# Relational layer: first half multiplied by quarters, turns one place later, ScalarE normalising a half later

## The reference

```python
B, N, D_IN, D_OUT, R = (8, 1024, 128, 128, 4)
rel_ids = jnp.arange(1, weight.shape[0] + 1, dtype=relation.dtype)
masks = (relation[None] == rel_ids[:, None, None, None]).astype(x.dtype)
h = jnp.einsum('rbnm,bmd->rbnd', masks, x)
y = jnp.einsum('rbnd,rdo->bno', h, weight)
y = y + bias
...
x = _layernorm(x + y, axis=-1)     # (x - mean) / sqrt(var + 1e-5)
```

## Time and profile before

| | |
|---|---|
| median of 3 runs | 127.29 us |
| the profiled execution, whole | 128.38 us |
| its span, first to last instruction | 126.6 us |
| PE busy | 104.6 us (83%) |
| DVE busy | 96.2 us (76%) |
| ACT busy | 83.4 us (66%) |
| POOL busy | 79.8 us (63%) |
| moved by DMA | 42.15 MB, 333 GB/s over the span |

### The profile page before, as it was taken

The page is one execution under the profiler, slowest core; times in us unless marked ns, Lnnn a source line. Parts: engine busy times, 40 slices in busy tenths (PEclk is TensorE's granted clock), DMA queues, the critical chain, the costliest instruction groups (busy, mean ns, idle before and its releaser), DMA issues.

```text
span 126.6 us, 1876 instructions
## 1 busy us (share of the span) xinstructions
PE 104.6 (83%) x551; PEld 85.0 (67%) x559; DVE 96.2 (76%) x243; ACT 83.4 (66%) x114; POOL 79.8 (63%) x76
## 2 busy tenths in 40 slices
PE   5933399989999789899999999999999999997100
PEld 2312288687878567678887887788879886896000
DVE  0249925277949999999999999999999997639820
ACT  4056780766649178699589939994999499951400
POOL 6008000067253989899989989999999899043510
PEclk9996557999999999999999999999999999999855
DMA  4999999999999999999999999999999700400620
GB/s 116 409 422 430 425 422 432 422 430 405 434 419 419 427 417 425 410 436 417 422 365 409 425 422 359 421 427 427 388 281 418 311 18 0 166 0 0 250 87 8
DMA packets 7362, 42.15 MB, mean 333 GB/s; under 512 B 819, under 2 KB 1206, under 8 KB 3254
## 3 DMA queue, kind: packets, MB, share of 16 engines
q1 hardware_dynamic: 7350, 42.01, 81.7%
HBM read 37.82 MB, written 4.19 MB: 332 GB/s over the span
## 4 chain that ended last, share of the span: by engine, by line
DMA 25%; DVE 22%; PE 18%; ACT 11%; POOL 11%; issue 6%; SPq 2%; DVEq 0%; POOLq 0%; ACTq 0%
DMA adj_sb<-in_adj_dram 25%; PE h_ps L187 13%; POOL scale L217 10%; ACT maskT L355 9%; DVE mask L426 6%; DVE stats L205 4%; DVE var_eps L214 4%; DVE total L440 3%; PE tp_ps L178 2%; PE y_ps L199 2%; DVE mean_var L210 2%; DVE out_sb L221 2%; ACT out_sb L374 1%; ACT h_sb L362 1%; SPq L244 1%
## 5 line engine op out<-in xcount | busy, mean ns | idle before, releaser
L355 ACT ACTIVATE maskT<-tp_ps 128x2048 fp32r<-128x2048 fp8e5 x32 | 59.7, 1873 | 8.1 <-PE tp_ps L178 8.1
L426 DVE TENSOR_SCALAR mask<-adj_sb 128x2048 uint8<-128x2048 uint32 x32 | 39.7, 1266 | 16.2 <-DMA adj_sb<-in_adj_dram 16.1
L217 POOL TENSOR_TENSOR scale<-var_eps,power 128x4 f32<-128x4 f32 (+1 forms) x17 | 44.3, 2608 | 0.6 <-DVE var_eps L214 0.6
L187 PE MATMUL h_ps<-maskT,x_hi 128*128 128x512 f32 (+1 forms) x136 | 35.7, 406 | 1.1 <-ACT maskT L355 0.9
L187 PE MATMUL h_ps<-maskT,x_lo 128*128 128x512 f32 (+1 forms) x136 | 33.8, 391 | 0.0
L178 PEld LDWEIGHTS tp_ps<-identity,mask 128*128 128x128 f32 x128 | 20.3, 204 | 13.8 <-DVE mask L426 10.2
L187 PEld LDWEIGHTS h_ps<-maskT,x_hi 128*128 128x128 f32 x136 | 24.7, 197 | 6.6 <-ACT maskT L355 2.3
L178 PE MATMUL tp_ps<-identity,mask 128*128 128x128 f32 x128 | 22.3, 300 | 7.9 <-DVE mask L426 7.8
L374 ACT ACTIVATE out_sb<-total,shift,scale 128x128 f32<-128x128 f32 x31 | 13.7, 488 | 19.8 <-POOL shift L319 19.8
L187 PEld LDWEIGHTS h_ps<-maskT,x_lo 128*128 128x128 f32 x136 | 23.5, 189 | 3.9
L199 PE MATMUL y_ps<-w_sb,h_sb 128*128 128x128 f32 x128 | 17.3, 277 | 1.6 <-ACT h_sb L362 1.3
(11 more groups left out here) (32 smaller groups left out, 33.3 us busy)
## 6 DMA issues: line engine op xcount, KB each, us to landing
adj_sb<-in_adj_dram SPq DMA_DIRECT2D x32, 1024.0 KB, 12.2
x_sb<-in_x_dram SPq DMA_DIRECT2D x8, 512.0 KB, 5.9
out_dram<-out_sb SPq DMA_DIRECT2D x7, 512.0 KB, 16.5
out_dram<-out_sb SPq DMA_DIRECT2D x1, 256.0 KB, 2.4
out_dram<-out_sb SPq DMA_DIRECT2D x2, 128.0 KB, 1.9
w_sb<-in_L_gnn_weight_dram SPq DMA_DIRECT2D x1, 64.0 KB, 6.5
bias_rows<-in_L_gnn_bias_dram SPq DMA_DIRECT2D x3, 0.5 KB
```

Of the source, the lines that this page charges most:

```text
L187: last = nc.tensor.matmul(h_ps[:, bank, 0:n], (x_hi, x_lo)[part][:, slot, t, :], maskT[:, places, t // WORD, t % WORD, :], start=(first an ...
L217: nc.gpsimd.tensor_tensor(scale[:, slot, tiles], var_eps[:, slot, tiles], power[:, tiles], ALU.pow).then_inc(done, by)
L355: nc.scalar.activation(maskT[:, u % NMT], turned_codes(u % NTP), ACT.Copy, accum_out=counts[:, u:u + 1]).then_inc(expanded, 1)
L426: nc.vector.tensor_scalar(mask[:, u % NMASK], adj_sb[:, u % NADJ].bitcast(u32), CAP, SET, ALU.min, ALU.mult).then_inc(masked, 1)
```

## The change

Several things move, and no arithmetic on the data is added or taken away.

- PE in the loop: a turn now stands behind the products that it stood ahead of. The order is hi_products(hf), turn(2hf+3), project_half(hf-1), lo_products(hf), turn(2hf+4).
- ACT: finish_half is that of half hf-3 instead of hf-2, and at the end the finishes stand between the copies.
- DVE: each pair of converts is one unit earlier in number (2hf+4 and 2hf+5), so that add and measure of a half stand ahead of one more convert. `find_others` stands ahead of the last whole add, and the flag is written ahead of the two last adds. `place_bias` stands ahead of convert(1).
- Half 0 goes by quarters: each quarter is multiplied behind its own turn, copied and projected before half 1 starts. Two stretches of idle matmuls (8 and 4) on a zero tile are added.
- `x_hi` and `x_lo` of batch 0 are made by POOL.
- The bias and the weight are loaded from ACT's queue, not SP's; x of the next batch is loaded one unit later.
- At the end PE's order is: first part of quarter 0, projection of half 14, second part of quarter 0, first part of quarter 1, the sum of counts, projection of quarter 0, second part of quarter 1, projection of quarter 1.

```diff
-            load_unit(1)
-            sp.wait_ge(bias_cleared, 1)
-            for q in PARTS:
-                sp.dma_start(bias_rows[q:q + 1, :], bias.unsqueeze(0)).then_inc(bias_loaded, 16)
-            sp.dma_start(w_sb[:, 0, :], weight[0]).then_inc(weights_loaded, 16)
-            for u in range(2, UNITS):
+            for u in range(1, UNITS):
                 load_unit(u)
-                if u % CH == 1 and u // CH + 1 < B:
+                if u % CH == (2 if u >= CH else 3) and u // CH + 1 < B:
                     load_batch(u // CH + 1)
-                if u == 3:
-                    load_batch(1)
...
             split_bias()
+            hi(0)
+            lo(0)
...
+            act.wait_ge(bias_cleared, 1)
+            for q in PARTS:
+                act.dma_start(bias_rows[q:q + 1, :], bias.unsqueeze(0)).then_inc(bias_loaded, 16)
+            act.dma_start(w_sb[:, 0, :], weight[0]).then_inc(weights_loaded, 16)
             expand(0)
-            act.wait_ge(topped, 1)
-            nc.scalar.activation(flat(x_hi[:, 0]), flat(x_top[:, :]).bitcast(fp32), ACT.Copy).then_inc(hi_made, 1)
             expand(1)
-            for hf in range(HALVES - 1):
-                if hf >= 1:
+            copy_quarter(0, 0)
+            expand(2)
+            copy_quarter(0, 1)
+            expand(3)
+            for hf in range(1, HALVES - 1):
+                if hf >= 2:
                     copy_half(hf - 1)
                 expand(2 * hf + 2)
                 expand(2 * hf + 3)
-                if hf >= 2:
-                    finish_half(hf - 2)
+                if hf >= 3:
+                    finish_half(hf - 3)
             copy_half(HALVES - 2)
+            finish_half(HALVES - 4)
+            copy_quarter(HALVES - 1, 0)
             finish_half(HALVES - 3)
-            copy_quarter(HALVES - 1, 0)
             copy_quarter(HALVES - 1, 1)
...
             convert(0)
             top(0)
-            convert(1)
-            dve.wait_ge(topped, 1)
-            take_lo(nc.vector, 0, 0, lo_made)
-            convert(2)
             place_bias()
-            convert(3)
+            for u in (1, 2, 3):
+                convert(u)
+            top(1)
             convert(4)
-            for hf in range(HALVES - 1):
-                for u in (2 * hf + 5, 2 * hf + 6):
+            convert(5)
+            for hf in range(1, HALVES - 1):
+                for u in (2 * hf + 4, 2 * hf + 5):
...
+            find_others()
             add_half(HALVES - 2)
             measure_half(HALVES - 2)
             finish_half(HALVES - 3)
-            find_others()
+            dve.wait_ge(flag_counted, 1)
+            nc.vector.tensor_copy(flag[:, :], tp_ps[0:1, 0, 0:1]).then_inc(flag_ready, 1)
...
             turn(0)
+            keep_warm(8)
+            hi_quarter(0, 0)
             turn(1)
+            lo_quarter(0, 0)
             turn(2)
-            for hf in range(HALVES - 1):
+            hi_quarter(0, 1)
+            lo_quarter(0, 1)
+            turn(3)
+            pe.wait_ge(weights_loaded, 16)
+            pe.wait_ge(bias_split, 4)
+            project_half(0)
+            keep_warm(4)
+            hi_products(1)
+            turn(4)
+            lo_products(1)
+            turn(5)
+            turn(6)
+            for hf in range(2, HALVES - 1):
+                hi_products(hf)
                 if 2 * hf + 3 < UNITS:
                     turn(2 * hf + 3)
-                hi_products(hf)
+                project_half(hf - 1)
+                lo_products(hf)
                 if 2 * hf + 4 < UNITS:
                     turn(2 * hf + 4)
-                if hf == 1:
-                    pe.wait_ge(weights_loaded, 16)
-                    pe.wait_ge(bias_split, 4)
-                if hf >= 1:
-                    project_half(hf - 1)
-                lo_products(hf)
-            products_quarter(HALVES - 1, 0)
+            hi_quarter(HALVES - 1, 0)
             project_half(HALVES - 2)
-            products_quarter(HALVES - 1, 1)
-            project_quarter(HALVES - 1, 0)
+            lo_quarter(HALVES - 1, 0)
+            hi_quarter(HALVES - 1, 1)
             pe.wait_ge(flag_step, 2)
             nc.tensor.matmul(tp_ps[0:1, 0, 0:1], above[:, 1:2], ones[:, 0:1], start=True, stop=True).then_inc(flag_counted, 1)
+            project_quarter(HALVES - 1, 0)
+            lo_quarter(HALVES - 1, 1)
             project_quarter(HALVES - 1, 1)
```

21 lines of the change are left out of this document (11 added, 10 removed).

## The result

The changed kernel takes 120.25 us, median of four executions (118.53 to 121.04), beside 127.31 us (126.42 to 127.34, four executions) for the kernel before on the same chip. The ratio is 0.9365, with a 95% interval of 0.927 to 0.946.

A forecast was written before the change was run, and what follows sets the result against it. Bound by data up to 37 us, by full DVE to 101.5, then DVE waits for PE. Start 1.8, loop nothing, end the rest: 5.0 summed, 4.9 taken, so 127.29 - 4.9 = 122.4 us, range 120.8 to 125.5.

The forecast's parts named there:

- The start: Data-bound stage: DVE work moves ahead of convert(10), convert(11) starts at 39.4 instead of 41.4; 1.8 us gained.
- The bias rival: Start, DVE: place_bias waits for a late bias ahead of 31 converts; 129 us, chance 0.05 including other slower causes.
- order of issue: Start, DMA: if loads land as issued, bias at about 15.5 and convert(1) at 19.4; the sum stays the same.
- The start has enough slack for the rest: Start: POOL's batch 0 work, half 0 by quarters, 12 idle matmuls and two PE waits cost nothing.
- The loop: From 37 to 101.5 us: DVE stays full at 12.0 us per batch, so nothing is gained.
- this sign (a period below 11.8): Loop, DVE: a batch period below 11.8 us would mean x_lo has slid off var_eps.
- The end: From add 12: PE in time, DVE's 1.73 us wait before add 13 goes, 0.35 of 2.01 stays before add 14.
- the walk: Timing of DVE and PE through the end, instruction by instruction: last finish at 116.3 instead of 121.22, 4.9 us.
- What follows the last finish: After DVE's last finish: the store, its landing and the end were claimed to stay, so no gain.
- ACT's finish is only the loudest wait: Loop: ACT's 19.8 us wait for POOL's shift stands beside a full DVE and does not set the stage's length.
- More than counted: unit 11 early: Start and end: unit 11 is there by 37.5 and PE keeps up; 120.5 to 121 us, chance 0.07.

The follow-up runs named there:

- the long execution: Second profiled execution of the changed kernel, nothing further edited: 120.83 us, span 119.1, DVE batches of 11.97 us.
- the short one: First profiled execution of the changed kernel, nothing further edited: 118.53 us, span 116.7, two DVE batches of 11.15 us.

## Why the prediction was off

**The start** held. convert(11) was at 39.3 and 39.5 for 39.4; x_lo met it in the long execution as written (until 40.9 was forecast, until 41.02 it was), and in the short one came behind it, at 41.03, and met var_eps instead (0.70). The bias rival did not come: place_bias began at 8.0 in the short execution and ended at 12.2, and a beginning at 20.0 was still in time by the prediction, as the timeline of all engines shows:

```profile
6.79 0.40 POOL L287 TENSOR_TENSOR bias_rest<-bias_rows 128x128 f32<-128x128 f32 x1 [4.15 <-DMA bias_rows<-in_L_gnn_bias_dram]
...
8.03 1.22 DVE L491 COPY bias_parts<-bias_rows 1x512 bf16<-1x512 bf16 x1 [0.29 <-POOL bias_fine L290]
9.27 2.49 DVE L491 COPY bias_parts<-bias_rest 1x512 bf16<-1x512 bf16 x1
...
12.22 2.36 DVE L429 TENSOR_SCALAR mask<-adj_sb 128x2048 uint8<-128x2048 uint32 x2
```

The bias landed at 6.8 on ACT's queue; it was 9.5 behind unit 1 before. The 15.5 that the prediction gave for order of issue had a wrong premise: ACT issued the bias from 1.50 to 2.6, when SP was at units 1 (1.72) and 2 (2.19), not behind unit 3. Its last piece was still issued behind unit 1 and landed 2.6 us ahead of where unit 1 landed before (9.4). By the Trainium skill, "DMA: Bandwidth & Descriptors", "Queues, rings and completion order", the engines take turns between queues: the trace agrees, 6.8.

"The start has enough slack for the rest ... I cost them at nothing" holds only where DVE sets the loop, as in the long execution. Where PE sets it, its start comes through to add 14 one to one, and in the chains of those traces PE's start goes back to convert(1) and the bias copies ahead of it. By the place of place_bias alone the median moves by 1.7 to 2.7 us, in part by more short executions.

**The loop** was costed at nothing, by two steps. "Turns one place later are needed by converts that are one unit lower in number, so that this cancels" hid that the turns' place is what keeps the converts' lead: the converts alone are worth nothing, with the turns 4 us. Whoever had taken the converts' move as the gain would have been wrong by all of it. "The 1.3 us per batch that x_lo costs through var_eps stays" is the first step that failed. The order on POOL does stay, but the amount doesn't: it is 1.28 us (1.45 - 0.17) in the long execution and 0.48 in the short one's first batches, since the pow ahead of x_lo gets through sooner or later between two converts. The prediction named this sign (a period below 11.8) and gave it no chance. With where x_lo falls at convert(11) it makes the 2.44 us between the two executions. It explains little of the median's miss if the six of ten executions at 120.6 to 121.0 are long ones, of which one was profiled. What decides whether an execution is long or short is not settled.

**The end** held: no wait ahead of add 13, 0.76 ahead of add 14 for the 0.35 written, the last finish 0.26 us ahead of its time in the long execution. 5.18 us came up to there, for the 4.9 of the walk.

**What follows the last finish** is the step that put the forecast out of its range. "What follows the last finish (the store, its landing, the end) stays" was taken as 5.4 us; it was 3.06. The flag's move was priced as the 0.1 to 0.2 us of its instruction on DVE, and not by what waits for the flag: five engines that read it and branch. On the long execution the two add up to what was measured, as they must, being read from it: 128.38 - 5.18 - 2.3 = 120.9, for 120.83. Without this term it would have been 123.2, beside the 123.5 forecast. From the median the forecast's own 4.9 and this term give 127.3 - 4.9 - 2.3 = 120.1, for 120.25; that it comes so close is partly luck, since the median lies between the two kinds of execution.

**The rivals.** That ACT's finish is only the loudest wait was held and shown. "More than counted: unit 11 early" gave 120.5 to 121, close to the right time for a wrong reason: unit 11 came at 39.3, not 37.5.

## What to carry to other kernels

Price an instruction that is moved by who waits for its result, the end of the program included: here 0.14 us on DVE stood for 2 us of five engines' endings. Two moves that form one ring through PE and DVE have to be judged together: the converts alone showed nothing, and with the turns 4 us. Where two engines are both nearly full, write down both paces (here 11.5 us per batch for PE, 11.15 or 11.97 for DVE), since removing one wait only brings up the other. And where two engines hold each other up at the scale of a tenth of a microsecond, give the period a range of its own, and read two profiled executions before arguing from one.

## What the runs showed of the hardware

- x_lo (2.40 us on POOL) holds up DVE's scalar instructions to its end: var_eps 0.17 becomes 1.45, a pair of finishes 0.57 becomes 1.18, a convert 1.23 becomes 2.78, a copy of 0.42 becomes 2.49. The measures (`stats`, `mean_var`) kept their 0.87 and 0.38. The other way round POOL's pow over 128x4 beside two converts was not held up to their end, nor did it hold them up: in the short execution it started at 54.87, 0.12 us ahead of the converts at 54.99, took 1.38 us, and a pair of converts kept its 2.35. The Trainium skill, "SBUF — State Buffer", section "Who interferes with whom", says of DVE's two-port modes, which tensor_scalar and copy can enter, that whoever issues first gets the ports shared with GpSimd for the whole instruction. x_lo behaves so here; the pow, by these rows, does not. Which mode DVE was in no run shows.
- A flag written 4.7 to 5.2 us ahead of the end of the last finish, so that most engines have begun to read it by then, goes with a stretch behind that finish of 2.7 to 3.9 us (fourteen traces), a flag written at that end with 4.8 to 5.4 (six).
- A drop of the granted clock in three slices of the start (clock 0.952 over the span for 0.991) left the median where it was (120.56 for 120.25) in a kernel none of whose four executions was short. Where PE sets the pace, a later start of PE came through whole (28.95 to 30.38 at half 2, 105.79 to 107.21 at add 14).
